# A fused vision tower on one core: the last unit's value products in another buffer, GpSimd's additions behind its last normalisation, output matrices scaled later, far coefficients at the front

## The chip, the cores and the metric

The kernel runs on one core of a Trainium2 chip. The core has a matmul engine (TensorE, PE in the profile), VectorE (DVE), ScalarE (ACT), GpSimd (POOL) and SyncE (SP), whose queue issues the DMAs. The engines run side by side and wait for each other through semaphores. The metric is the device time of one execution in microseconds (us), lower is better. Before the change the median of three runs is 881.12 us (879.34 to 882.15).

## The reference

Everything is float32. Three stages follow one another:

1. A tokenizer over 64 images of 64 channels by 64 x 64 pixels. Each 4 x 4 patch is averaged, `reduce_feats = x.mean((3, 5))`. The averages are normalised and make queries, the 16 pixels of the patch are normalised and make keys and values, and each patch attends to its own 16 pixels with 8 heads: `attn = softmax(q*scale . k)`, `aggre = attn . v`, `h = reduce_feats + aggre @ proj_w.T + proj_b`. That gives 256 tokens of 64 channels for each image.
2. A linear recurrence over the 256 tokens of each image, two states x and z per channel: `x_new = s*x - dsa*z + fx`, `z_new = ds*x + s*z + fz`, with forces made from the tokens by a matrix B. Then `gelu(y @ C + u @ D)`, times its sigmoid, plus the input, and a layer norm.
3. A small network of a shared path and 4 experts of which each token takes 2, and a last layer norm.

## The kernel before

**Units and steps.** Two images lie on the 128 partitions, so the first stage has 32 units (0 to 31), and it is pipelined by hand: step n does the value side of unit n, the key side of unit n + 1 and the first sums of unit n + 2. Each engine has its program written out in the order of its work; nothing is rescheduled. Four units of x fit in `arena`.

**One unit.** GpSimd adds the 16 pixels of each patch in four halvings (lines 497 to 507), after `patch_sums_first` has waited for x. ScalarE makes the means. TensorE makes query means (912, 917), pixel means and squares (924), keys and values (952) into two rings of PSUM. VectorE makes the variance of the queries (`query_var`, 1328), scales them (1333), multiplies keys by queries (`key_products`, 1349) into `prodk`, and scales the scores and takes their maximum (1356, 1363). GpSimd subtracts the maximum (`shift_scores`, 586), ScalarE takes the exponential (`expo`, 708), VectorE sums it (1367) and inverts the sum (1372), GpSimd makes the weights (`weigh_scores` 592, `norm_scores` 597). SyncE spreads them over the channels with eight DMAs into `wbc` (545). VectorE multiplies the values by them (`value_products`, 1380) into `prodv`, four quarters in the order 0, 2, 1, 3; GpSimd adds 4 of the 16 pixels to 4 others (`add_pixels`, 604). TensorE projects the remaining 12 and sums them (`project`, 991), and VectorE adds mean and bias and stores the tokens in `hT` (`tokens`, 1387).

**`prodv` is one buffer.** Value products of unit n wait until `project(n - 1)` has read it (`dve.wait_ge(projected_mm, u)`). In the steady steps projection n - 1 comes before them.

**The second stage begins inside the first.** The tokens are split into halves h = 0 (units 0 to 15) and h = 1. `drive(h, b)` (1006) makes the forces of block b of 4 recurrence steps in four blocks, `forcing` (746) copies them to `z[h]` in SBUF, `scan_ahead` and `scan_on` (1398, 1404) run the recurrence within chunks of L = 16 tokens, and `carry` joins the 16 chunks of an image by four jumps (1449 to 1456), whose steps need powers of the 16-step matrix, `far_steps` (1429, 1432). `scale_out` (738) makes 32 scaled copies of the matrix C with which `from_before` (1100) adds the carried states to the outputs. For h = 0 all of that needs only units 0 to 15, so `drive(0, 0)` to `drive(0, 3)` and part of the scan stand in the last two steps; h = 1 begins when the tokens of unit 31 are there. Step 30 is the last but one: it has keys of unit 31, no sums of a further unit.

**At the start** VectorE prepares constants and does the patch sums of unit 0 itself (483 to 489); GpSimd begins with the patch sums of unit 1 once these are done.

## Time and profile before

| | us |
|---|---|
| median of 3 runs | 881.12 |
| the profiled execution | 881.01 |
| its span on the core | 879.2 |
| PE busy | 838.2 |
| DVE busy | 717.9 |
| POOL busy | 524.4 |
| ACT busy | 483.5 |

The busy time is summed over the whole span. The first stage ends at about 556 us, the recurrence at about 598 us, and the third stage fills the rest. Since each stage has its own limits, the shares of the whole say little of an edit in one place; the order of time around it does. The granted clock of TensorE was 0.99 over the span.

### The profile page before, as it was taken

Reading aid. Unit: us, or ns where it says so; the run is one execution under the profiler, and the core shown is the slowest. Engines: PE = TensorE matmul, PEld = TensorE weight load, DVE = VectorE, ACT = ScalarE, POOL = GpSimd, SP = SyncE. Lnnn points to the kernel's source line nnn. Section 1 sums busy time; section 2 is a strip of 40 time slices with the busy share of each in tenths; the row PEclk is TensorE's granted clock in tenths of the full one; section 3 lists DMA queues with packets and bytes.
Section 4 is the critical chain, followed back from the end, with each engine's and each line's share of the span. In section 5 each row is a group of like instructions: output and inputs, shape, how many; then the busy total and the mean of one; then the engine's idle time right before and its main releaser. Section 6 shows DMA issues by size and latency. Waiting matters only on the chain.

```text
span 879.2 us, 23479 instructions
## 1 busy us (share of the span) xinstructions
PE 838.2 (95%) x9144; PEld 360.6 (41%) x9144; DVE 717.9 (82%) x1189; ACT 483.5 (55%) x782; POOL 524.4 (60%) x387
## 2 busy tenths in 40 slices
PE   5799999999999999999999997898999999999996
PEld 2134334344344343343343443464444444444442
DVE  5788888888888888888888888894788788788785
ACT  3646456455454464564554554358666566566562
POOL 2699999999999999999999964101121121121110
PEclk9999999999999999999999998999999999999999
DMA  9588998989989989999899764000000000000000
GB/s 374 158 240 252 260 283 245 263 267 260 275 250 260 286 242 259 278 250 263 256 253 264 217 168 111 2 2 2 0 13 13 25 13 13 25 13 13 25 13 36
DMA packets 70560, 141.60 MB, mean 161 GB/s; under 512 B 5440, under 2 KB 5440, under 8 KB 69440
## 3 DMA queue, kind: packets, MB, share of 16 engines
q1 hardware_dynamic: 70464, 140.21, 55.4%
q8 instruction: 74, 1.21, 0.6%
q14 instruction: 22, 0.18, 0.1%
HBM read 68.88 MB, written 4.19 MB: 83 GB/s over the span
## 4 chain that ended last, share of the span: by engine, by line
PE 39%; POOL 37%; issue 7%; DVE 7%; ACT 4%; DMA 3%; SPq 2%; POOLq 1%; DVEq 0%; ACTq 0%
POOL sb_rows L497 11%; POOL sb_prodv L604 7%; POOL sb_rows L502 6%; PE ring L1207 5%; POOL sb_wgt L592 4%; PE ring L1177 4%; POOL sb_rows L504 3%; POOL sb_score L586 3%; PE ring L952 3%; PE bank_ms L1219 3%; DMA sb_wbc<-sb_wgt 3%; SPq L545 2%; PE bank_ms L924 2%; PE qp L991 2%; PE qp L1162 2%
## 5 line engine op out<-in xcount | busy, mean ns | idle before, releaser
L952 PE MATMUL ring<-sb_arena,sb_wqkv 64*64 64x512 f32 x2048 | 254.1, 599 | 2.3 <-DVE sb_prodk L1349 1.5
L1380 DVE TENSOR_TENSOR sb_prodv<-ring,sb_wbc 128x1024 f32<-128x1024 f32 x128 | 151.8, 1206 | 43.6 <-DMA sb_wbc<-sb_wgt 25.4
L1349 DVE TENSOR_TENSOR sb_prodk<-ring,sb_qbuf 128x1024 f32<-128x1024 f32 x128 | 150.6, 1218 | 22.3 <-PE ring L952 16.8
L648 POOL TENSOR_TENSOR sb_parts_q<-sb_arena,sb_const 128x512 fp32r<-128x512 f32 x15 | 15.6, 1039 | 245.6 <-DVE sb_arena L1585 194.4
L497 POOL TENSOR_TENSOR sb_rows<-sb_arena 128x2048 f32<-128x2048 f32 x31 | 142.2, 4586 | 15.8 <-DVE sb_sum L489 15.8
L692 ACT ACTIVATE sb_xsq<-sb_arena 128x2048 f32<-128x2048 f32 x64 | 118.6, 1901 | 2.0 <-DMA sb_arena<-x 2.0
L952 PEld LDWEIGHTS ring<-sb_arena,sb_wqkv 64*64 64x64 f32 x2048 | 66.3, 132 | 115.6 <-issue 72.3
L991 PEld LDWEIGHTS qp<-sb_prodv,sb_tok_w 64*64 64x64 f32 x3072 | 93.1, 137 | 40.4 <-issue 40.2
L991 PE MATMUL qp<-sb_prodv,sb_tok_w 64*64 64x128 f32 x3072 | 98.8, 276 | 5.2 <-POOL sb_prodv L604 5.2
L604 POOL TENSOR_TENSOR sb_prodv<-sb_prodv 128x256 f32<-128x256 f32 x128 | 92.8, 735 | 10.7 <-DVE sb_prodv L1380 10.7
L663 ACT ACTIVATE sb_means<-sb_sum 128x256 f32<-128x256 f32 x32 | 13.3, 416 | 146.9 <-POOL sb_sum L507 143.1
L502 POOL TENSOR_TENSOR sb_rows<-sb_rows 128x1024 f32<-128x1024 f32 x31 | 73.9, 2383 | 2.4
L924 PE MATMUL bank_ms<-sb_arena,sb_const 128*32 128x512 f32 x512 | 63.3, 613 | 2.2 <-issue 2.2
L924 PE MATMUL bank_ms<-sb_prodk,sb_const 128*32 128x512 f32 x512 | 61.6, 598 | 1.8 <-DVE sb_prodk L1349 1.8
L924 PE MATMUL bank_sq<-sb_xsq,sb_const 128*32 128x512 f32 x512 | 60.8, 592 | 0.0
L450 ACT ACTIVATE sb_arena<-ring,sb_rest_w 128x512 f32<-128x512 f32 x72 | 49.0, 682 | 7.6 <-PE ring L1167 2.8
L586 POOL TENSOR_TENSOR sb_score<-sb_score,sb_smx 128x512 f32<-128x512 f32 x32 | 40.8, 1276 | 15.8 <-DVE sb_smx L1363 15.4
L1177 PE MATMUL ring<-sb_arena,sb_rest_w 64*128 64x512 f32 x144 | 48.2, 607 | 0.0
L592 POOL TENSOR_TENSOR sb_wgt<-sb_score,sb_rstd 128x512 f32<-128x512 f32 x32 | 41.1, 1285 | 9.9 <-ACT sb_score L708 8.6
L1207 PE MATMUL ring<-sb_prodk,sb_rest_w 128*64 128x512 f32 x192 | 45.9, 598 | 0.0
L673 ACT ACTIVATE sb_qstat<-sb_qstat,sb_const 128x256 f32<-128x256 f32 x32 | 16.3, 509 | 47.1 <-DVE sb_qstat L1328 47.1
L597 POOL TENSOR_TENSOR sb_wgt<-sb_wgt,sb_srz 128x512 f32<-128x512 f32 x32 | 40.9, 1279 | 1.8 <-DVE sb_srz L1372 1.5
(248 smaller groups left out, 1450.1 us busy)
## 6 DMA issues: line engine op xcount, KB each, us to landing
sb_arena<-x SPq DMA_DIRECT2D x64, 1024.0 KB, 7.4
sb_wbc<-sb_wgt SPq DMA_DIRECT2D x256, 256.0 KB, 5.7
out<-sb_arena SPq DMA_DIRECT2D x16, 256.0 KB, 2.0
sb_rest_w<-rest_w SPq DMA_DIRECT2D x1, 950.5 KB, 21.3
sb_const<-const SPq DMA_DIRECT2D x1, 264.5 KB, 3.0
sb_tok_w<-tok_w SPq DMA_DIRECT2D x1, 260.5 KB, 2.9
sb_const<-const SPq DMA_DIRECT2D x1, 256.0 KB, 21.6
```

The lines of the kernel that those rows point to most:

```text
L497: eng.tensor_tensor(rows[:, :, :, :], pix[:, :, 0:8], pix[:, :, 8:16], ALU.add).then_inc(sum8_ready, 1)
L502: eng.tensor_tensor(rows[:, :, 0:4], rows[:, :, 0:4], rows[:, :, 4:8], ALU.add).then_inc(sum4_ready, 1)
L592: pool.tensor_tensor(wgt[:, :], score[:, :], rstd[:, :], ALU.mult).then_inc(weights_raw, 1)
L604: pool.tensor_tensor(part[:, :, N_SUM - N_PRE:N_SUM], part[:, :, N_SUM - N_PRE:N_SUM], part[:, :, N_SUM:N_PIX], ALU.add).then_inc(pixels_a ...
L692: act.activation(xsq[:, half], x[:, m, b].rearrange("p c n -> p (c n)"), ACT.Square).then_inc(pixels_squared, 1)
L924: mm = pe.matmul(bank[32 * c:32 * c + 32, :], what, src[c], start=(b == 0), stop=(b == 1))
L952: mm = pe.matmul(ring[slot][C * half:C * half + C, i, :], image_block(w, i), x[C * i:C * i + C, m, half, c], start=True, stop=True)
L991: mm = pe.matmul(qp[C * i:C * i + C, half, 3 * PT:4 * PT], image_block(projw, half), prodv[rows_of, i, n, :], start=(n == 0), stop=(n == N ...
L1177: pe.matmul(pair[m][:, :], ew1[rows, e, :], h2[rows, i % 3, :], start=True, stop=True).then_inc(ring_mm, 1)
L1207: mm = pe.matmul(bank[C * h:C * h + C, :], ew2[:, 2 * q + h, :], h1e[:, im, 2 * q + h], start=True, stop=True)
L1349: dve.tensor_tensor(by_pixel(prodk[:, c]), by_pixel(ring[c % 2][:, :, :]), q[:, :, None, :].to_broadcast([P, 2, N_PIX, G32]), ALU.mult).th ...
L1380: dve.tensor_tensor(prodv[:, :, :, G32 * c:G32 * (c + 1)], by_pixel(ring[k % 2][:, :, :]), by_pixel(wbc[:, c]), ALU.mult).then_inc(values_ ...
```

## The change

Five edits, all but one in the last two steps of the first stage:

- Unit 31 writes its value products into `prodk` (`products_of`, `prod_last`), whose last user is the scores matmul of unit 31; `project(31)` and the additions read them there. `value_products(31, 0)` waits for `scores_mm` instead of `projected_mm`. TensorE's `project(30)` moves behind `values(31, 1)` and `drive(0, 2)`; VectorE's `tokens(30)` moves behind the first two value products of unit 31.
- GpSimd in step 30: `add_pixels(30, 0)` before `shift_scores(31)`, `add_pixels(30, 1)` between it and `weigh_scores(31)`, and nothing between that and `norm_scores(31)`.
- ScalarE: `scale_out` moves from step 30, ahead of `expo(31)`, to the last step, between the forces of blocks 2 and 3.
- VectorE: the twelve instructions of `far_steps` move from the last step to the front, behind the patch sums of unit 0 and ahead of `query_var(0)`.
- VectorE: ten recurrence steps instead of eight stand ahead of `tokens(31)`: 5 before the first value product, 2 behind the second, 3 behind the fourth.

```diff
@@ gpsimd, step @@
-                if nxt:
+                if nxt and not nxt2:
+                    add_pixels(n, 0)
                     shift_scores(n + 1)
-                add_pixels(n, 0)
-                if nxt:
+                    add_pixels(n, 1)
                     weigh_scores(n + 1)
-                add_pixels(n, 1)
-                if nxt:
                     norm_scores(n + 1)
...
@@ scalar, step @@
                 if not nxt:
-                    forcing(0)
+                    forcing(0, range(N_BLOCK - 1))
+                    scale_out()
+                    forcing(0, range(N_BLOCK - 1, N_BLOCK))
...
-                if nxt and not nxt2:
-                    scale_out()
@@ tensor, last_step @@
                 drive(0, 1)
                 values(n, m, 0)
-                project(n - 1, 0, N_SUM)
                 values(n, m, 1)
                 drive(0, 2)
+                project(n - 1, 0, N_SUM)
                 values(n, m, 2)
@@ vector, value_products @@
                 if k == 0:
-                    dve.wait_ge(projected_mm, u)
-                dve.tensor_tensor(prodv[:, :, :, G32 * c:G32 * (c + 1)], by_pixel(ring[k % 2][:, :, :]),
+                    if isinstance(u, int) and u == UNITS - 1:
+                        dve.wait_ge(scores_mm, UNITS)
+                    else:
+                        dve.wait_ge(projected_mm, u)
+                dve.tensor_tensor(products_of(u)[:, :, :, G32 * c:G32 * (c + 1)], by_pixel(ring[k % 2][:, :, :]),
@@ vector @@
-            EARLY, BEFORE_TOKENS = 5, 9
+            EARLY, BETWEEN, BEFORE_TOKENS = 6, 8, 11
+
+            for level in range(3):
+                far_steps(level)
             query_var(0)
@@ vector, last_step @@
                 for j in range(1, EARLY):
                     scan_ahead(0, j)
                     scan_on(0, j)
-                tokens(n - 1, (m - 1) % NF)
                 value_products(n, m, 0)
                 value_products(n, m, 1)
-                for level in range(3):
-                    far_steps(level)
+                for j in range(EARLY, BETWEEN):
+                    scan_ahead(0, j)
+                    scan_on(0, j)
+                tokens(n - 1, (m - 1) % NF)
                 value_products(n, m, 2)
                 value_products(n, m, 3)
-                for j in range(EARLY, BEFORE_TOKENS):
+                for j in range(BETWEEN, BEFORE_TOKENS):
```

VectorE at the front, before: the last patch sum of unit 0 (`sb_sum`), then the variance and scaling of the first queries and the first key products.

```order
L489 TENSOR_TENSOR sb_sum<-sb_rows 128x128 [waits sum2_ready]
L1328 TENSOR_TENSOR sb_qstat<-qp,sb_qstat 128x256 [waits q_mean_squared]
L1333 TENSOR_TENSOR sb_qraw<-qp,sb_qrstd 128x256 [waits q_ready,q_rstd_ready]
L1349 TENSOR_TENSOR sb_prodk<-ring,sb_qbuf 128x1024 [waits scores_mm,q_ready,keys_mm]
L1349 TENSOR_TENSOR sb_prodk<-ring,sb_qbuf 128x1024 [waits keys_mm]
```

The same place after the change (the twelve instructions go on in the same pattern; `sb_far` holds the powers, `sb_cacc` a temporary).

```order
L495 TENSOR_TENSOR sb_sum<-sb_rows 128x128 [waits sum2_ready]
L1347 TENSOR_SCALAR sb_cacc<-sb_cv,sb_cz 128x2
L1347 TENSOR_SCALAR sb_cacc<-sb_cv 128x2
L1350 SCALAR_TENSOR_TENSOR sb_far<-sb_cz,sb_cacc 128x2 [waits far_step]
L1350 SCALAR_TENSOR_TENSOR sb_far<-sb_cz,sb_cv,sb_cacc 128x2
L1347 TENSOR_SCALAR sb_cacc<-sb_far 128x2 [waits far_step]
```

Between the patch sum and the variance now stand three levels of two `TENSOR_SCALAR` and two `SCALAR_TENSOR_TENSOR`; each of the latter reads two operands in SBUF.

GpSimd from the end of step 29 to the end of its first stage, before (`sb_wgt` holds the weights, `sb_prodv` the value products).

```order
L604 TENSOR_TENSOR sb_prodv<-sb_prodv 128x2x4x32 [waits values_weighted] x2
L586 TENSOR_TENSOR sb_score<-sb_score,sb_smx 128x512 [waits score_max_ready]
L604 TENSOR_TENSOR sb_prodv<-sb_prodv 128x2x4x32 [waits values_weighted]
L592 TENSOR_TENSOR sb_wgt<-sb_score,sb_rstd 128x512 [waits weights_spread2,weights_spread1,weights_spread3,weights_spread0,scores_exp]
L604 TENSOR_TENSOR sb_prodv<-sb_prodv 128x2x4x32 [waits values_weighted]
L597 TENSOR_TENSOR sb_wgt<-sb_wgt,sb_srz 128x512 [waits inverse_sum_ready,weights_raw]
L604 TENSOR_TENSOR sb_prodv<-sb_prodv 128x2x4x32 [waits values_weighted] x6
```

The same place after.

```order
L610 TENSOR_TENSOR sb_prodv<-sb_prodv 128x2x4x32 [waits values_weighted] x3
L592 TENSOR_TENSOR sb_score<-sb_score,sb_smx 128x512 [waits score_max_ready]
L610 TENSOR_TENSOR sb_prodv<-sb_prodv 128x2x4x32 [waits values_weighted]
L598 TENSOR_TENSOR sb_wgt<-sb_score,sb_rstd 128x512 [waits weights_spread2,weights_spread1,weights_spread3,weights_spread0,scores_exp]
L603 TENSOR_TENSOR sb_wgt<-sb_wgt,sb_srz 128x512 [waits inverse_sum_ready,weights_raw]
L610 TENSOR_TENSOR sb_prodv<-sb_prodv 128x2x4x32 [waits values_weighted] x2
L610 TENSOR_TENSOR sb_prodk<-sb_prodk 128x2x4x32 [waits values_weighted] x4
```

The second `sb_wgt` instruction, the normalisation, now follows the first directly, and the four additions of unit 31 work on `sb_prodk`.

VectorE in the last step, before: tokens of unit 30 (`sb_hT`), the first two value products, then the far coefficients.

```order
L1387 SCALAR_TENSOR_TENSOR sb_hT<-qp,sb_bqkv,sb_means 128x16x16 [waits projected_mm]
L1380 TENSOR_TENSOR sb_prodv<-ring,sb_wbc 128x32x32 [waits projected_mm,weights_spread0,values_mm]
L1380 TENSOR_TENSOR sb_prodv<-ring,sb_wbc 128x32x32 [waits weights_spread2,values_mm]
L1429 TENSOR_SCALAR sb_cacc<-sb_cv,sb_cz 128x2
L1429 TENSOR_SCALAR sb_cacc<-sb_cv 128x2
L1432 SCALAR_TENSOR_TENSOR sb_far<-sb_cz,sb_cacc 128x2 [waits far_step]
```

After: the last recurrence step of the middle pair, the tokens of unit 30, and value products 3 and 4 of unit 31.

```order
L1428 SCALAR_TENSOR_TENSOR sb_arena<-sb_arena,sb_sv 128x256 [waits force_ready,scan_step0]
L1434 SCALAR_TENSOR_TENSOR sb_arena<-sb_arena,sb_sv 128x256 [waits scan_step0]
L1417 SCALAR_TENSOR_TENSOR sb_hT<-qp,sb_bqkv,sb_means 128x16x16 [waits projected_mm]
L1410 TENSOR_TENSOR sb_prodk<-ring,sb_wbc 128x32x32 [waits weights_spread1,values_mm]
L1410 TENSOR_TENSOR sb_prodk<-ring,sb_wbc 128x32x32 [waits weights_spread3,values_mm]
```

The tokens moved from ahead of the first value product to between the second and the third, and the far coefficients are gone from there.

## Rows read from the trace of the kernel before

**Rows 1.** the page, the chain that ended last, shares of the span by engine

```profile
PE 39%; POOL 37%; issue 7%; DVE 7%; ACT 4%; DMA 3%; SPq 2%; POOLq 1%; DVEq 0%; ACTq 0%
```

**Rows 2.** stretches: busy us (instructions) by engine, granted clock, DMA share, GB/s

```profile
300.00:316.00 16.00, 16.00 (x232) 6.55 (x227) 13.77 (x17) 8.39 (x12) 15.39 (x12) 1.00 0.91 262
551.00:556.00 5.00, 4.52 (x96) 4.30 (x96) 3.20 (x8) 0.00 (x0) 0.26 (x2) 0.66 0.01 3
```

**Rows 3.** GpSimd in order of time at the front: start us, us, instruction, idle before

```profile
16.27 4.53 POOL L497 TENSOR_TENSOR sb_rows<-sb_arena 128x2048 f32<-128x2048 f32 x1 [15.82 <-DVE sb_sum L489]
20.87 2.37 POOL L502 TENSOR_TENSOR sb_rows<-sb_rows 128x1024 f32<-128x1024 f32 x1
23.32 1.27 POOL L504 TENSOR_TENSOR sb_rows<-sb_rows 128x512 f32<-128x512 f32 x1
...
30.88 1.27 POOL L586 TENSOR_TENSOR sb_score<-sb_score,sb_smx 128x512 f32<-128x512 f32 x1 [5.47 <-DVE sb_smx L1363]
```

**Rows 4.** VectorE in order of time at the front

```profile
15.82 0.29 DVE L489 TENSOR_TENSOR sb_sum<-sb_rows 128x128 f32<-128x128 f32 x1
19.24 0.42 DVE L1328 TENSOR_TENSOR sb_qstat<-qp,sb_qstat 128x256 f32<-128x256 f32 x1 [3.12 <-ACT sb_qstat L669]
```

**Rows 5.** VectorE in order of time, the far coefficients in the last step

```profile
545.17 0.22 DVE L1429 TENSOR_SCALAR sb_cacc<-sb_cv 128x2 f32<-128x2 f32 x1
545.42 0.57 DVE L1432 SCALAR_TENSOR_TENSOR sb_far<-sb_cz,sb_cacc 128x2 f32<-128x2 f32 x1
545.91 0.21 DVE L1432 SCALAR_TENSOR_TENSOR sb_far<-sb_cz,sb_cv,sb_cacc 128x2 f32<-128x2 f32 x1
```

**Rows 6.** GpSimd in order of time, the last units

```profile
501.78 1.28 POOL L597 TENSOR_TENSOR sb_wgt<-sb_wgt,sb_srz 128x512 f32<-128x512 f32 x1
...
528.87 1.27 POOL L586 TENSOR_TENSOR sb_score<-sb_score,sb_smx 128x512 f32<-128x512 f32 x1 [8.51 <-DVE sb_smx L1363]
...
534.12 1.28 POOL L597 TENSOR_TENSOR sb_wgt<-sb_wgt,sb_srz 128x512 f32<-128x512 f32 x1
535.35 1.77 POOL L604 TENSOR_TENSOR sb_prodv<-sb_prodv 128x256 f32<-128x256 f32 x2
...
545.20 0.77 POOL L604 TENSOR_TENSOR sb_prodv<-sb_prodv 128x256 f32<-128x256 f32 x1 [0.40 <-DVE sb_prodv L1380]
...
550.03 0.89 POOL L604 TENSOR_TENSOR sb_prodv<-sb_prodv 128x256 f32<-128x256 f32 x1 [0.40 <-DVE sb_prodv L1380]
```

**Rows 7.** VectorE in order of time, the last units

```profile
509.16 1.23 DVE L1380 TENSOR_TENSOR sb_prodv<-ring,sb_wbc 128x1024 f32<-128x1024 f32 x1 [0.31 <-DMA sb_wbc<-sb_wgt]
...
532.17 1.04 DVE L1367 TENSOR_REDUCE sb_ssm<-sb_score 128x32 f32<-128x512 f32 x1 [1.03 <-ACT sb_score L708]
533.24 0.35 DVE L1372 RECIPROCAL sb_srz<-sb_ssm 128x32 f32<-128x32 f32 x1
...
534.59 1.09 DVE L1398 SCALAR_TENSOR_TENSOR sb_arena<-sb_arena,sb_sv 128x256 f32<-128x256 f32 x1
...
542.27 0.67 DVE L1387 SCALAR_TENSOR_TENSOR sb_hT<-qp,sb_bqkv,sb_means 128x256 f32<-128x256 f32 x1 [2.63 <-PE qp L991]
...
547.60 2.35 DVE L1380 TENSOR_TENSOR sb_prodv<-ring,sb_wbc 128x1024 f32<-128x1024 f32 x2
...
555.64 0.65 DVE L1387 SCALAR_TENSOR_TENSOR sb_hT<-qp,sb_bqkv,sb_means 128x256 f32<-128x256 f32 x1 [1.69 <-PE qp L991]
```

**Rows 8.** one line of the scan: durations ns, first and last start us

```profile
L1398 DVE SCALAR_TENSOR_TENSOR sb_wbc<-sb_wbc,sb_sv x14: 477/485/489, 569.7 to 581.6; 128x256 f32<-128x256 f32 x14
```

**Rows 9.** ScalarE in order of time, the last two steps

```profile
523.88 7.74 ACT L738 ACTIVATE sb_arena<-sb_rest_w,sb_cz 128x64 f32<-128x64 f32 x32
531.53 0.61 ACT L708 ACTIVATE sb_score<-sb_score 128x512 f32<-128x512 f32 x1
```

**Rows 10.** TensorE in order of time, last projection and end of the scan

```profile
551.07 4.52 PE L991 MATMUL qp<-sb_prodv,sb_tok_w 64*64 64x128 f32 x96 [3.94 <-POOL sb_prodv L604]
...
590.38 1.87 PE L1100 MATMUL ring<-sb_xsq,sb_arena 64*64 64x128 f32 x60 [1.96 <-DVE sb_xsq L1456]
```

More of the change, by code:

```diff
@@ L198, in image_block, with products_of @@
             return w[C * i:C * i + C, C * i:C * i + C]
+        prod_last = prodk[:, :, :, :].rearrange("p c i n -> p (c i n)").rearrange("p (i n t) -> p i n t", i=2, n=N_PIX)
+        def products_of(u):
+            return prod_last if isinstance(u, int) and u == UNITS - 1 else prodv
         x = arena[:, :].rearrange("p (m b c n) -> p m b c n", m=NF, b=2, c=NC)
@@ L738, in scale_out, with forcing @@
                         act.activation(dst[:, j], out_mat, ACT.Copy, scale=cz[:, j + 1, o:o + 1]).then_inc(scaled_out, 1)
-            def forcing(h):
+            def forcing(h, blocks):
                 act.wait_ge(coefs, N_COEFS)
-                for b in range(N_BLOCK):
+                for b in blocks:
                     act.wait_ge(drive_mm, N_BLOCK * h + b + 1)
@@ L771, in _ @@
             pipeline(act, step, UNITS)
-            forcing(1)
+            forcing(1, range(N_BLOCK))
             def norm_sq(i):
@@ L1324, in _, with far_steps, last @@
             first_patch_sums(dve, 1)
+            def far_steps(level):
+                def last(acc):
+                    return (cz, cv)[acc][:, L] if level == 0 else far[:, acc, level - 1]
+                if level > 0:
+                    dve.wait_ge(far_step, 4 * level)
+                for acc in range(2):
+                    dve.tensor_scalar(cacc[:, acc, 0], last(1), last(acc)[:, 1:2], None, ALU.mult).then_inc(far_step, 1)
+                dve.wait_ge(far_step, 4 * level + 2)
+                for acc in range(2):
+                    dve.scalar_tensor_tensor(far[:, acc, level], last(0), last(acc)[:, 0:1], cacc[:, acc, 0],
+                                             ALU.mult, ALU.add).then_inc(far_step, 1)
             def query_var(u):
```

24 lines of the change are left out of this document (11 added, 13 removed).

## The prediction

> **What bounds the kernel now.** I read first the chain that ended last by engine: TensorE and GpSimd share it, the others have little [rows 1]. Then stretches. In a steady stretch of 16 us GpSimd is busy 15.39 us, and TensorE counts as busy throughout while its matmuls are pipelined [rows 2]; so in the first stage GpSimd has almost no slack, and a delay of its first unit is not made up later. Third, the order of time of GpSimd and VectorE at the front [rows 3, 4] and of all engines in the last two steps [rows 5 to 10]. There the reader is to see a chain of short waits: ScalarE's exponential of unit 31 stands behind 32 scalings [rows 9], VectorE sits idle for the projection of unit 30 before it may overwrite `prodv` (2.63 us) and again for the projection of unit 31 (1.69 us) [rows 7], and TensorE waits 3.94 us for the last addition and 1.96 us for the last carry [rows 10].
>
> The sum is made on the profiled execution: 881.01 us, which is its span of 879.2 and 1.8 around it, and 0.11 below the median of the runs shown. Times below are on the clock of the trace of before; the delay at the front, where there is one, shifts all that follows alike and is added at the end.
>
> **The exponential and the normalisation, 1.5 us.** `shift_scores(31)` ends at 528.87 + 1.27 = 530.14 [rows 6], but the exponential begins at 531.53, behind scalings that took 7.74 us from 523.88 [rows 9]. With these moved it runs 530.2 to 530.8. VectorE's sum of it had 1.03 us of idle ahead of it [rows 7], so VectorE was free at 531.14: sum and reciprocal come 1.03 earlier and end at 533.24 + 0.35 - 1.03 = 532.56. Before, the normalisation did not start on the reciprocal's end (533.59) but at 534.12, behind an addition; now nothing is between. It starts at 532.6, 1.5 us earlier, and ends at 533.9. The two additions that now stand before it (0.73 each) lie in the wait for the scores' maximum, 8.51 us [rows 6], and beside the exponential.
>
> **The spread of the weights sets the first value product.** Its price is in unit 29, where no wait but the DMA's stood before the product: normalisation over at 501.78 + 1.28 = 503.06 [rows 6], product at 509.16, released by the DMA [rows 7]: 6.1 us. So `value_products(31, 0)` can start at 533.9 + 6.1 = 540.0 and not before. It started at about 542.8 (tokens of unit 30 from 542.27, after the projection). The freed buffer thus brings 2.8 us, no more, and VectorE has a new idle of about 1 us for the DMA, because five recurrence steps from 533.5 at 0.915 us each ((581.6 - 569.7) / 13 [rows 8]), with some waits for GpSimd, end at about 539.0.
>
> **From there to the last projection, 2.9 us.** Two value products 2.35 [rows 7], two recurrence steps 1.83 and 0.2 for one wait behind an addition, tokens of unit 30 (0.5 to the next start), two products 2.35: 540.0 + 7.2 = 547.2. Before, the last pair began at 547.60 and ended at 549.95, and the projection started at 551.07, 1.1 later. Now it starts at 548.2, 2.9 earlier. TensorE's projection of unit 30 is finished long before 544 in either case, since its additions end at about 535.5.
>
> **The recurrence, 1.8 us more.** Ten steps instead of eight are ahead of the tokens of unit 31, so 2 x 0.915 = 1.83 us are gone from VectorE's work behind them. VectorE is busy from 555.64 until it releases TensorE at 590.38. TensorE had 1.96 us of slack there [rows 10] and its own work starts with the tokens too, so the gain is the smaller of 1.83 and 1.96. Together the last steps give 2.9 + 1.8 = 4.7 us. The scalings, now behind the forces of block 2 (copied by about 537.6: the exponential's end at 530.8 and then three blocks, each some 2.2 us of matmuls and copying), run to 545.3 and the forces of block 3 to 546.8; the first matmul of half 1 wants them at about 553.6, so they cost nothing; without that cover they cost up to their 7.74.
>
> What of the 4.7 is loose: the last projection took 4.52 us, and the granted clock was 0.66 over 551 to 556 [rows 2], so about 0.34 x 5 / 0.5 = 3.4 us of it were at the lower of the two levels. All at the upper, it would be 1.7 shorter; all at the lower, about 1.1 longer. I leave it as it was. With 0.5 for the other starts, the gain is 3.3 to 6.5.
>
> **The far coefficients at the front, a loss of 5.7 us.** Their own time is about 2.6 us (the second of the twelve started at 545.17, the value products behind them at 547.60 [rows 5, 7], one more ahead), and they go into a gap of 3.12 us ahead of the first query variance [rows 4]: by that alone they are free. But two rows show what a `SCALAR_TENSOR_TENSOR` with both operands in SBUF does beside GpSimd. At 545.42 one on 2 elements took 0.57 us and its twin 0.21; GpSimd's addition ran 545.20 to 545.97, and the first of the two ended at 545.99 [rows 5, 6]. At 534.59 a recurrence instruction took 1.09 instead of 0.485; GpSimd's normalisation ended at 535.40, and it ended 0.28 after that [rows 6 to 8]. Each waited for GpSimd's running instruction to end. At the front GpSimd starts its patch sum of unit 1 at 16.27, for 4.53 us [rows 3]. VectorE's last patch sum ends at 16.11, its first `SCALAR_TENSOR_TENSOR` of the far steps would start 0.3 us later at 16.4, the same distance as at 545.12 to 545.42, so after GpSimd again. It waits until 20.80. Its twin passes in the gap to 20.87. Level 1 needs two short instructions first, meets the second patch sum (20.87, 2.37) and waits until about 23.3; level 2 meets the third (23.32, 1.27) and waits until about 24.7; two short ones more and `query_var(0)` starts at 24.9 instead of 19.24: 5.7 us late. Behind it hang the query's scaling, the key products, the scores and `shift_scores(0)`, for which GpSimd had been idle 5.47 us waiting on VectorE [rows 3], so the whole delay arrives there, and with GpSimd at 15.39 of 16 us nothing takes it back.
>
> The nearest rows bound this loss on both sides: 0 if no such wait arises, and for the upper end VectorE losing every gap until GpSimd runs out of patch sums at about 25.4, plus two free levels of 0.8 (2.4 us for three [rows 5, 7]): 27.0, or 7.8 us late. I take 5.7 because both rows show VectorE getting in as soon as GpSimd's instruction ends.
>
> The rule in the Trainium skill, page "SBUF — State Buffer", section "Who interferes with whom", goes further than these rows: besides VectorE instructions with two SBUF inputs it names `tensor_scalar` from SBUF to SBUF, in a two-port mode, as one that shares the port pair with GpSimd and blocks or is blocked for a whole instruction. No row here shows that for a `TENSOR_SCALAR`: the one at 545.17 was already running. By that rule it would come out as the second rival.
>
> **Sum.** 881.01 - 4.7 + 5.7 = 882.0 us. A difference under 0.3%, 2.6 us, is what this kernel's measurement cannot tell from none; the forecast is within it.
>
> **Rivals.**
> - No block at the front. The far steps fit the 3.12 us gap, VectorE's first one beats GpSimd to it, or the waits are short. For it: a margin of only 0.13 us between GpSimd's start (16.27) and VectorE's. Against it: the same margin at 545.2 did not help. Time: 881.0 - 4.7 = 876.3, faster.
> - VectorE loses more gaps: also its `TENSOR_SCALAR` instructions wait. Level 1's pair waits for 23.3 and its next for 24.7, level 2's for 25.5, and 0.8 us later, at 26.3, the variance starts: 7.1 late, 7.8 at the bound. Time: 881.0 - 4.7 + 7.1 = 883.4, up to 884.1, slower. It decides from the point where one level more than in my count is left over when GpSimd's third sum ends.
> - The moved scalings turn into the wait. If block 2's forces come only behind the projection, the scalings start near 548 and block 3's forces end at 557.2, and drive and recurrence of half 1 begin there. This leaves a gain of 0.8 instead of 4.7, and 881.0 - 0.8 + 5.7 = 885.9, slower. It decides from a start of the scalings after 544.3; TensorE's `drive(0, 2)` stands ahead of the projection, which speaks against it.
>
> **How the numbers follow.** Forecast 0.60, no block 0.16, more gaps lost 0.20, scalings 0.04. The likeliest one's own range is 880 to 883.6 (gain 3.3 to 6.5, loss 5.6 to 6). The whole range, 876.0 to 884.3, takes in the first two rivals. Faster by over 2.6 us is almost only the no-block case and a lucky clock: 0.17. Slower by over 2.6 (from 883.7): half of the second rival, all of the third and a little of the forecast: 0.17. The same: 0.66.
>
> **What would show it.** At the front: the first `SCALAR_TENSOR_TENSOR` of the far steps lasting over 4 us and ending with GpSimd's first patch sum, `query_var(0)` near 24.9, and every later start of GpSimd's patch sums 5.7 us later than before; if it stands at 19.2, that step is wrong and 876 follows. In the last steps: the normalisation of unit 31 1.5 us nearer to its score maximum, an idle of about 1 us of VectorE for the weights' DMA, no idle for the projection of unit 30, the last projection starting 15.6 us after the start of that normalisation (551.07 - 534.12 = 16.95 before), and TensorE's 1.96 us before the last `from_before` almost gone. The forecast is wrong if first-stage delays are absorbed between the units, or if the last projection finds the clock at another level for all of its length.

## The result and the profile after

| | kernel before | changed kernel |
|---|---|---|
| time, median | 880.59 us (878.81 to 882.73, 7 runs) | 884.71 us (883.27 to 888.05, 7 runs) |
| ratio, 95% interval | | 1.0055 (1.004 to 1.007) |
| profiled execution, span | 879.2 us | 881.5 us (883.27 us in all) |
| measured again (e16 below) | 880.15 us | 884.21 us, 1.0050 (1.0036 to 1.0065) |

It is slower by 4.1 us. I had forecast 882.0 us, no measurable difference, and at most 884.3. The profiled execution is the fastest of the seven, so its differences to before (+2.3 us) understate the median; where the rest lies is shown with e16.

In the chain by engine GpSimd and VectorE each hold three points less than in [rows 1] and TensorE seven more:

```profile
PE 46%; POOL 34%; issue 8%; DVE 4%; DMA 3%; SPq 2%; ACT 2%; POOLq 1%; DVEq 0%
```

The front, VectorE in order of time (start us, us, instruction, idle before), answering to [rows 4]:

```profile
16.39 4.39 DVE L1350 SCALAR_TENSOR_TENSOR sb_far<-sb_cz,sb_cacc 128x2 f32<-128x2 f32 x1
20.70 0.21 DVE L1350 SCALAR_TENSOR_TENSOR sb_far<-sb_cz,sb_cv,sb_cacc 128x2 f32<-128x2 f32 x1
20.94 2.40 DVE L1347 TENSOR_SCALAR sb_cacc<-sb_far 128x2 f32<-128x2 f32 x2
23.38 1.30 DVE L1350 SCALAR_TENSOR_TENSOR sb_far<-sb_far,sb_cacc 128x2 f32<-128x2 f32 x2
24.72 0.77 DVE L1347 TENSOR_SCALAR sb_cacc<-sb_far 128x2 f32<-128x2 f32 x2
...
25.79 0.42 DVE L1355 TENSOR_TENSOR sb_qstat<-qp,sb_qstat 128x256 f32<-128x256 f32 x1
```

and GpSimd, answering to [rows 3]:

```profile
16.24 4.52 POOL L503 TENSOR_TENSOR sb_rows<-sb_arena 128x2048 f32<-128x2048 f32 x1 [15.79 <-DVE sb_sum L495]
20.83 2.36 POOL L508 TENSOR_TENSOR sb_rows<-sb_rows 128x1024 f32<-128x1024 f32 x1
23.27 1.26 POOL L510 TENSOR_TENSOR sb_rows<-sb_rows 128x512 f32<-128x512 f32 x1
24.61 0.72 POOL L513 TENSOR_TENSOR sb_sum<-sb_rows 128x256 f32<-128x256 f32 x1
38.23 1.28 POOL L592 TENSOR_TENSOR sb_score<-sb_score,sb_smx 128x512 f32<-128x512 f32 x1 [12.90 <-DVE sb_smx L1390]
```

Read the two side by side. The first `SCALAR_TENSOR_TENSOR` ends at 20.78, GpSimd's first sum at 20.76. Level 1's two `TENSOR_SCALAR`s end at 23.34, GpSimd's second sum at 23.19; the pair of `SCALAR_TENSOR_TENSOR`s at 24.68 and the third sum at 24.53; level 2's `TENSOR_SCALAR`s at 25.49 and the fourth sum at 25.33. So at each of GpSimd's four ends the waiting pair gets through, and the next pair starts 0.11 us after the next sum has begun (20.94 against 20.83, 23.38 against 23.27, 24.72 against 24.61) and has to wait for it. `query_var(0)` starts at 25.79, 6.55 us late. GpSimd's first shift starts at 38.23, 7.35 us late: the other 0.8 us is TensorE's, which had no matmul from 22.5 to 29.6; its granted clock fell to the lower of its two levels at 25.8 (0.50, which is 1.2 of 2.4 GHz), and it began the key products there. The stretches of the idle and of the key products, engines' busy us and granted clock as in [rows 2]:

```profile
20.00:28.00 8.00, 2.47 (x24) 0.42 (x16) 6.49 (x12) 1.19 (x3) 5.09 (x4) 0.86 0.81 334
28.00:32.00 4.00, 2.39 (x12) 0.75 (x16) 3.29 (x4) 1.41 (x3) 0.00 (x0) 0.50 0.02 4
```

The tail, on GpSimd (answering to [rows 6]), VectorE [rows 7] and TensorE [rows 10]:

```profile
524.18 1.28 POOL L603 TENSOR_TENSOR sb_wgt<-sb_wgt,sb_srz 128x512 f32<-128x512 f32 x1 [0.18 <-DVE sb_srz L1399]
...
539.89 1.27 POOL L603 TENSOR_TENSOR sb_wgt<-sb_wgt,sb_srz 128x512 f32<-128x512 f32 x1 [0.39 <-DVE sb_srz L1399]
...
555.81 0.90 POOL L610 TENSOR_TENSOR sb_prodk<-sb_prodk 128x256 f32<-128x256 f32 x1 [0.40 <-DVE sb_prodk L1410]
```

```profile
532.73 1.22 DVE L1410 TENSOR_TENSOR sb_prodv<-ring,sb_wbc 128x1024 f32<-128x1024 f32 x1 [1.38 <-DMA sb_wbc<-sb_wgt]
...
548.46 2.35 DVE L1410 TENSOR_TENSOR sb_prodk<-ring,sb_wbc 128x1024 f32<-128x1024 f32 x2 [2.13 <-issue]
...
553.40 2.33 DVE L1410 TENSOR_TENSOR sb_prodk<-ring,sb_wbc 128x1024 f32<-128x1024 f32 x2
...
559.76 0.65 DVE L1417 SCALAR_TENSOR_TENSOR sb_hT<-qp,sb_bqkv,sb_means 128x256 f32<-128x256 f32 x1 [0.94 <-PE qp L1004]
...
564.98 0.42 DVE L1446 TENSOR_TENSOR sb_xsq<-sb_arena 128x256 f32<-128x256 f32 x1
```

```profile
543.11 2.80 PE L1004 MATMUL qp<-sb_prodv,sb_tok_w 64*64 64x128 f32 x96
549.74 3.69 PE L965 MATMUL ring<-sb_arena,sb_wqkv 64*64 64x512 f32 x16 [3.83 <-DVE sb_prodk L1410]
...
556.85 2.85 PE L1004 MATMUL qp<-sb_prodk,sb_tok_w 64*64 64x128 f32 x96 [1.78 <-POOL sb_prodk L610]
```

How late each is against before, in us: normalisation of unit 30 +6.47 (524.18 against 517.71), normalisation of unit 31 +5.77, first value product of unit 31 +5.68, last pair of them +5.80, last projection +5.78, tokens of unit 31 +4.12, end of the recurrence +2.28 (564.98 against 562.70), end +2.3. So the last normalisation gained 1.58 on the 7.35; nothing more was gained up to the last projection; the projection itself took 2.85 instead of 4.52 because here it found the full clock (the lower level lay from 548.1 to 554.9, ahead of it, and in before from 551.8 to 555.3, across it); and the two recurrence steps moved ahead gave 1.84. The last projection starts 16.96 us after the start of that normalisation; I had said 15.6, and before it was 16.95.

### The profile page after: what moved, and what is told of

Read it like the earlier page. It is cut to its first block, busy times and chain, and to the rows that moved or that the text cites. A ratio compares the mean times of both kernels' runs of the same rounds, so it can differ in the third digit from the quotient of the medians.

```text
span 881.5 us, 23480 instructions
## 1 busy us (share of the span) xinstructions
PE 836.6 (95%) x9144; PEld 357.6 (41%) x9144; DVE 725.1 (82%) x1189; ACT 483.6 (55%) x782; POOL 524.5 (60%) x387
## 4 chain that ended last, share of the span: by engine, by line
PE 46%; POOL 34%; issue 8%; DVE 4%; DMA 3%; SPq 2%; ACT 2%; POOLq 1%; DVEq 0%
POOL sb_rows L503 11%; POOL sb_rows L508 6%; POOL sb_prodv L610 6%; PE ring L965 6%; PE ring L1220 5%; PE ring L1190 4%; POOL sb_rows L510 3%; POOL sb_wgt L598 3%; PE bank_ms L937 3%; PE bank_ms L1232 3%; POOL sb_score L592 3%; DMA sb_wbc<-sb_wgt 3%; PE qp L1004 2%; PE qp L1175 2%; SPq L551 2%
## 5 line engine op out<-in xcount | busy, mean ns | idle before, releaser
L1410 DVE TENSOR_TENSOR sb_prodv<-ring,sb_wbc 128x1024 f32<-128x1024 f32 x124 | 147.1, 1206 | 43.7 <-PE ring L965 24.9
L661 POOL TENSOR_TENSOR sb_parts_q<-sb_arena,sb_const 128x512 fp32r<-128x512 f32 x15 | 15.6, 1039 | 243.7 <-DVE sb_arena L1604 194.4
L1004 PEld LDWEIGHTS qp<-sb_prodv,sb_tok_w 64*64 64x64 f32 x2976 | 86.6, 133 | 33.7 <-issue 33.7
L610 POOL TENSOR_TENSOR sb_prodv<-sb_prodv 128x256 f32<-128x256 f32 x124 | 89.9, 735 | 7.2 <-DVE sb_prodv L1410 7.2
L1004 PE MATMUL qp<-sb_prodv,sb_tok_w 64*64 64x128 f32 x2976 | 92.2, 269 | 0.0
```

The lines of the kernel that those rows point to most:

```text
L610: pool.tensor_tensor(part[:, :, N_SUM - N_PRE:N_SUM], part[:, :, N_SUM - N_PRE:N_SUM], part[:, :, N_SUM:N_PIX], ALU.add).then_inc(pixels_a ...
L1004: mm = pe.matmul(qp[C * i:C * i + C, half, 3 * PT:4 * PT], image_block(projw, half), products_of(u)[rows_of, i, n, :], start=(n == 0), sto ...
L1410: dve.tensor_tensor(products_of(u)[:, :, :, G32 * c:G32 * (c + 1)], by_pixel(ring[k % 2][:, :, :]), by_pixel(wbc[:, c]), ALU.mult).then_in ...
```

## The experiments

Medians; the ratio is to runs of the kernel before on the same chip, with its 95% interval. "Gap" is the place ahead of `score_scale(0)`, where VectorE waits 2.05 us for TensorE and GpSimd is idle. The runs of one kernel scatter by 2 to 11 us, and the intervals are 2 to 5 us wide, so differences under about 2 us between two kernels are not settled by the medians; smaller ones are read from the traces. The twelve instructions, 1.3 us in the expectations, take 2.3 us by themselves (e5).

| run | far coefficients | tail | us | ratio |
|---|---|---|---|---|
| e1 | last step | changed | 878.17 | 0.9976 (0.9961 to 0.9992) |
| e2 | front | before | 886.17 | 1.0064 (1.0045 to 1.0083) |
| e3 | gap | changed | 875.56 | 0.9944 (0.9928 to 0.9960) |
| e4 | gap | before | 878.33 | 0.9981 (0.9966 to 0.9996) |
| e5 | front, GpSimd held | changed | 874.54 | 0.9942 (0.9915 to 0.9970) |
| e6 | level 0 front, rest gap | changed | 877.72 | 0.9964 (0.9941 to 0.9987) |
| e7 | last step | products only | 880.02 | 0.9997 (0.9978 to 1.0015) |
| e8 | last step | additions, scaling only | 878.35 | 0.9973 (0.9961 to 0.9985) |
| e9 | gap | scalings last | 876.71 | 0.9963 (0.9949 to 0.9977) |
| e10 | gap | additions as before | 876.53 | 0.9946 (0.9929 to 0.9964) |
| e11 | gap | recurrence 7, 2, 2 | 873.85 | 0.9926 (0.9905 to 0.9946) |
| e12 | gap | scalings last, 5, 3, 3 | 877.92 | 0.9978 (0.9963 to 0.9993) |
| e13 | gap | transfers by chunk | 877.23 | 0.9972 (0.9961 to 0.9983) |
| e14 | gap | by chunk, 5, 2, 4 | 879.28 | 0.9991 (0.9975 to 1.0008) |
| e15 | gap | scaling as before | 876.59 | 0.9967 (0.9951 to 0.9984) |
| e16 | front | changed | 884.21 | 1.0050 (1.0036 to 1.0065) |

**e1, e2, e3, e4: the front against the tail.** Of the kernels e1 and e3 have the changed tail, e2 and e4 that of before. The place of three lines is all that differs:

```diff
@@ e3: the changed kernel, VectorE
-            for level in range(3):
-                far_steps(level)
             query_var(0)
 ...
             key_products(0, 0, 3)
+            for level in range(3):
+                far_steps(level)
             score_scale(0)
@@ e1: instead, in last_step, behind value_products(n, m, 1)
+                for level in range(3):
+                    far_steps(level)
```

> The changed kernel with the far coefficients back in the last step, behind the second value product; everything else as changed. Theory A (the front costs 6.5 to 7.3 us and the tail gains about 3 to 4): query_var(0) starts at 19.2 again and the time is 880.6 - 3.5 = about 877.1 (876.3 to 878.2). Rival B (the tail itself lost, by the slower transfer of the weights and the clock, and the stretch of stage 1 had taken back most of the front's loss): the time is 880 to 883.

> The kernel before with only the far coefficients moved to the front, ahead of query_var(0). Theory A: query_var(0) 6.5 late, GpSimd's first shift 7.3 late, and of that 0 to 0.9 taken back over stage 1; the last step saves the 1.3 us of the twelve instructions at most: 880.6 + 6.4 less 0 to 1.3 = 885.7 to 887.0. Rival B (stage 1 absorbs): 881 to 883.

> The changed kernel with the twelve instructions of the far coefficients between the first unit's last key product and its score_scale, where VectorE waits 2.05 us for TensorE and GpSimd is idle. Theory A: they take 1.3 us of those 2.05 us, nothing is late at the front, and the time is 876 to 878, by up to 1.3 us below the one with the coefficients in the last step. Rival C (any TENSOR_SCALAR chain at the front costs its own length): 878 to 879. Rival B: 880 to 883.

> The kernel before with only the far coefficients moved, to the same gap ahead of score_scale(0). Theory A: nothing lost at the front; in the last step 1.3 us of VectorE's work goes, but there it lay between the second value product and the wait for the third's sums, so it gains 0 to 1.3: 879.3 to 880.6. If the place at the front costs by itself, over 881.

Theory A holds, B falls: the tail alone is 2.1 us faster, the front alone 5.9 us slower. The front costs more against the gap, since the last step is rid of the twelve instructions in both: 7.8 us with the tail as before (e4 to e2), 9.1 with the changed tail (e3 to the changed kernel). Three places of the same twelve instructions with the tail as before: 886.2, 880.3 (the kernel before) and 878.3; with the changed tail: 884.7, 878.2 and 875.6. C falls as well: in the gap they cost nothing, `score_scale(0)` starts 9.89 us after `query_var(0)` in e3 and 9.81 in before. In e2's trace TensorE's granted clock was 0.50 for all of 28 to 38, longer than in the changed kernel's, and the first shift was 9.5 us late, not 7.35. The profile is of e2's longest run, so this is its upper end (VectorE, query variance and score scale):

```profile
25.99 0.42 DVE L1342 TENSOR_TENSOR sb_qstat<-qp,sb_qstat 128x256 f32<-128x256 f32 x1
...
38.56 0.69 DVE L1370 TENSOR_TENSOR sb_score<-bank_ms,sb_rstd 128x512 f32<-128x512 f32 x1 [3.76 <-PE bank_ms L924]
```

**e5: is it GpSimd?** One wait on GpSimd, ahead of its first patch sums:

```diff
+            pool.wait_ge(far_step, 12)
             patch_sums_first(pool, 1, 1)
```

> The changed kernel, far coefficients at the front as changed, but GpSimd waits for the twelfth of them before it starts its first patch sums. Theory A (what costs is GpSimd's running additions and nothing else): the twelve instructions take 2.1 us in all (0.2 each), GpSimd starts near 18.1 instead of 16.2 and ends its sums by 27.1, still ahead of its first shift at 30, query_var(0) starts by 19.2 and the time is that of the kernel with the coefficients in the gap, 875.6 (875 to 877). Rival D (GpSimd's late start is passed on, one for one): 877.3 to 878. Rival E (the place at the front costs by itself, whatever GpSimd does): 883 to 885.

```profile
16.36 0.22 DVE L1351 SCALAR_TENSOR_TENSOR sb_far<-sb_cz,sb_cacc 128x2 f32<-128x2 f32 x1
...
16.75 0.36 DVE L1348 TENSOR_SCALAR sb_cacc<-sb_far 128x2 f32<-128x2 f32 x2
17.14 0.35 DVE L1351 SCALAR_TENSOR_TENSOR sb_far<-sb_far,sb_cacc 128x2 f32<-128x2 f32 x2
...
18.89 0.43 DVE L1356 TENSOR_TENSOR sb_qstat<-qp,sb_qstat 128x256 f32<-128x256 f32 x1 [0.61 <-ACT sb_qstat L683]
```

The same instructions at the same place take 0.2 us each, 2.3 us in all, and fit the gap of 3.12 us; `query_var(0)` starts at 18.89. The time is that of e3. So the whole loss is GpSimd running beside them, D and E fall, and GpSimd's later start (18.36) costs nothing that shows.

**e6: one level.** `far_steps(0)` at the front, levels 1 and 2 in the gap.

> The changed kernel with only the first level of the far coefficients (four instructions) at the front, the other two levels in the gap ahead of score_scale(0). Theory A: the first SCALAR_TENSOR_TENSOR ends with GpSimd's first sum, at 20.8, query_var(0) starts at 21.0 instead of 18.5 to 19.2, 1.8 to 2.5 us late: 877.4 to 878.2 against 875.6 with all in the gap. Rival: each instruction pays a share of the 6.5 us (a third for a third): 2.2 us as well, but then spread over the four and not in the first.

```profile
16.38 4.48 DVE L1350 SCALAR_TENSOR_TENSOR sb_far<-sb_cz,sb_cacc 128x2 f32<-128x2 f32 x1
...
20.92 0.41 DVE L1355 TENSOR_TENSOR sb_qstat<-qp,sb_qstat 128x256 f32<-128x256 f32 x1
```

One instruction pays for all of it, 4.48 us. The median is 2.2 us above e3 as expected, but GpSimd's first shift was 5.1 us later than in e3 (35.32 against 30.20) though `query_var(0)` was only 2.44 later: TensorE, starved again, worked on the key products at a granted clock of 0.50 from 26 to 32. Its runs scatter from 873.3 to 883.2, and the profile (881.2) is from near the top of that range.

**e7, e8: the tail in its two parts.** e7 is before with `products_of`, the order of TensorE's `last_step` and the recurrence in 5, 2, 3 steps; e8 is before with the order of GpSimd's additions and the moved `scale_out` only (all as in the change's diff).

> The kernel before with only the products' part: the last unit's products in prodk, tokens(30) and project(30) behind the first two value products, two recurrence steps moved ahead; GpSimd's additions, the scaling and the far coefficients as before. If the first value product of the last unit is then bound by the transfer of the weights (7.3 us after the normalisation at 535.4, as in the changed kernel's trace), it starts at 542.7, where it started at 542.78 before: nothing there, and only the 1.8 us of the recurrence steps: 880.3 - 1.8 = 878.5. If the transfer takes 5.8 us, it starts at 541.2 and 1.5 us more come: 877.0. Forecast 877.0 to 878.8.

> The kernel before with only GpSimd's additions moved behind and ahead of the last normalisation and the scaling moved later; products, order and far coefficients as before. The last normalisation starts 1.5 us earlier, and since project(30) waits for GpSimd's additions behind it, tokens(30) and the first value product come 1.5 us earlier too, if the weights' transfer allows: 880.3 - 1.5 = 878.8. If the gain needs the new buffer, 880.3. Both parts together and no far coefficients moved were 878.2, so one of the two parts brings nothing on top of the other.

```profile
538.71 2.36 DVE L1403 TENSOR_TENSOR sb_prodk<-ring,sb_wbc 128x1024 f32<-128x1024 f32 x2 [0.46 <-issue]
540.99 0.22 DVE L1340 TENSOR_SCALAR sb_cacc<-sb_cv,sb_cz 128x2 f32<-128x2 f32 x1
...
545.25 0.65 DVE L1410 SCALAR_TENSOR_TENSOR sb_hT<-qp,sb_bqkv,sb_means 128x256 f32<-128x256 f32 x1
545.74 2.33 DVE L1403 TENSOR_TENSOR sb_prodk<-ring,sb_wbc 128x1024 f32<-128x1024 f32 x2
...
553.92 0.65 DVE L1410 SCALAR_TENSOR_TENSOR sb_hT<-qp,sb_bqkv,sb_means 128x256 f32<-128x256 f32 x1 [2.77 <-PE qp L997]
```

The early normalisation alone brings 1.7 us (e8). The buffer with its two recurrence steps brings nothing that the medians show (e7, where the interval leaves room for 1.9 us), and nothing on top of the early normalisation (e1, 878.2 against 878.35). e7's trace says why the buffer brings nothing. The first value product starts early, 5.60 us after the normalisation's end (533.11), but what follows it on VectorE is now the far coefficients (2.56 us) and two recurrence steps, and then the second pair starts 12.6 us after the normalisation's end where it was 12.2 in before. Without the far coefficients there the changed tail brings 2.8 us (e4 to e3), but that is not the buffer either: the last pair starts 12.2 us after the normalisation in e3 and 11.1 in e4, which has the old buffer. By their traces the gain is the normalisation 1.5 us nearer to its shift, the two recurrence steps, and a last projection of 2.85 us against 5.40, less this 1.1. The 2.1 and 2.8 us of the tail with and without the coefficients in it do not differ beyond the scatter.

**e9, e10, e15: which edit makes the normalisation early, and what does the scaling cost?**

```diff
@@ e9: e3, ScalarE in the last step
-                    forcing(0, range(N_BLOCK - 1))
-                    scale_out()
-                    forcing(0, range(N_BLOCK - 1, N_BLOCK))
+                    forcing(0, range(N_BLOCK))
+                    scale_out()
```

e10 is e3 with GpSimd's additions, e15 e3 with ScalarE's scaling as in the kernel before.

> The changed kernel with the far coefficients in the gap ahead of score_scale(0), and the 32 scalings of the output matrices behind all four blocks of forces, not ahead of the last. In the changed kernel's trace the first value product of the last unit started 7.3 us after the normalisation's end, in the runs with the scalings elsewhere 5.6 to 5.8. Theory F (the scalings beside the weights' transfer hold it up): it starts 5.6 to 5.8 us after, the idle of 2.1 us is gone, and the time is up to 1.5 us below the 875.6 of the same kernel with the scalings ahead of the last block: 874.1 to 875. Theory G (the transfer's own scatter, or another cause in the order): 7.3 again and 875.6. Both if the scalings' 7.7 us do not delay the forces of half 1.

> The changed kernel with the far coefficients in the gap, and GpSimd's additions in the order of before (shift, add, weigh, add, normalise). The exponential is early here, the additions stand between again. By the trace of before an addition took 0.73 and the normalisation waited behind one; by the forecast's count 0.5 of the 1.5 us of the normalisation's gain comes from the additions (534.12 against the reciprocal's end at 533.59) and 1.0 from the scalings: 875.6 + 0.5 = 876.1, and no more than 877.1. If the additions are all of it: 877.1.

> The changed kernel with the far coefficients in the gap and the scalings back where they were before, ahead of the exponential of unit 31. The exponential then waits for them: the normalisation of unit 31 1.0 us later (1.03 us of idle of VectorE ahead of the sum, in the trace of before). Theory: 875.6 + 1.0 = 876.6. If the first value product then starts 5.7 us after the normalisation instead of 7.3, that gives back 1.5: 875.0 to 875.6.

From the start of the shift to the start of the normalisation of unit 31 it is 3.81 us in e3, 3.92 in e10 and 4.87 in e15 (5.25 in before): put back alone, the scaling costs 1.1 and the additions 0.1, not 0.5, and both together 1.4. So the moved scaling brings nearly all of it, and the moved additions bring 0.4 only where the scaling stays (5.25 to 4.87). Kernels with both edits scatter from 3.66 to 3.95, so the 0.1 is not told from nothing. Theory F falls: with no scaling beside the transfer the first value product of e9 still starts 7.3 us after the normalisation (540.70 against 533.43), and the late scaling makes TensorE wait 1.33 us for the forces of half 1. e15 surprised: its normalisation is later, but the product starts 5.66 us after it, so both come out within a microsecond.

```profile
540.16 2.36 DVE L1410 TENSOR_TENSOR sb_prodk<-ring,sb_wbc 128x1024 f32<-128x1024 f32 x2 [0.50 <-issue]
```

**e13, e14: the order of the transfers.** SyncE issues four transfers for a pair of chunks; e13 swaps its two loops, e14 adds one recurrence step behind the last value product.

```diff
-                    for i in range(2):
-                        for c in VALUE_ORDER[k:k + 2]:
+                    for c in VALUE_ORDER[k:k + 2]:
+                        for i in range(2):
```

> The changed kernel with the far coefficients in the gap, and the four transfers of a pair of chunks issued chunk by chunk (both halves of the first chunk, then both of the second) instead of half by half. Theory H (the first value product of the last unit waits for the third of four transfers to land, and that is the 7.3 us): it is now the second of four, one issue of 0.75 us and about 1 us of transfer earlier, so the product starts by 5.6 us after the normalisation, the idle of 2.1 us shrinks to under 0.5, and the time is 0 to 1.5 us under 875.6. Rival (the wait is not for the transfer): 7.3 again, 875.6.

> As the one before, and one recurrence step more behind the last value product, ahead of the tokens of unit 31 (four where three were). It needs the forces of block 3, there by about 549. VectorE had 0.9 to 2.6 us of idle ahead of those tokens, so the step of 0.92 us is free: 0.9 below the time of the one before. If the forces of block 3 are late, nothing.

```profile
541.16 1.22 DVE L1410 TENSOR_TENSOR sb_prodk<-ring,sb_wbc 128x1024 f32<-128x1024 f32 x1
544.41 1.23 DVE L1410 TENSOR_TENSOR sb_prodk<-ring,sb_wbc 128x1024 f32<-128x1024 f32 x1 [2.04 <-DMA sb_wbc<-sb_wgt]
...
548.22 2.34 DVE L1410 TENSOR_TENSOR sb_prodk<-ring,sb_wbc 128x1024 f32<-128x1024 f32 x2
```

```profile
545.69 1.99 PE L965 MATMUL ring<-sb_arena,sb_wqkv 64*64 64x512 f32 x8 [2.17 <-DVE sb_prodk L1410]
...
551.68 4.52 PE L1004 MATMUL qp<-sb_prodk,sb_tok_w 64*64 64x128 f32 x96 [2.54 <-POOL sb_prodk L610]
```

Theory H is right on the wait and wrong on its worth. The first product starts 5.07 us after the normalisation (536.09), without idle: it did wait for the transfer. But the second waits until 8.3 us, as late as in e4, TensorE idles in between and falls to the lower level (eight matmuls 1.99 instead of 1.09, the projection 4.52 instead of 2.85), and the time is 1.7 us worse than e3. e14 is unclear: in its trace the recurrence ends 24.4 us after the normalisation against 25.4 in e13, the microsecond that was expected at that place, but its median is 2 us above e13's. Part of the answer is under e11: a third extra step arrives at TensorE as 0.3 us. Where the rest went is not shown.

**e11, e12: a better version.** `EARLY, BETWEEN, BEFORE_TOKENS` is 8, 10, 12 in e11 (before it 6, 8, 11); 6, 9, 12 with e9's scaling in e12.

> The changed kernel with the far coefficients in the gap and the recurrence of half 0 moved further ahead: 7 steps before the first value product (5 as changed), 2 before the tokens of unit 30 (2), 2 behind the last value product (3), so that one more is done before the tokens of unit 31. Two of the steps fit the idle of 2.1 us ahead of the first value product (1.83 us). If that idle is a wait and not time that VectorE itself needs, nothing else moves and the end of the recurrence comes 0.92 us earlier: 875.6 - 0.9 = 874.7. If the last projection or the forces of block 3 are late, 875.6; if the idle was not free, 877.4.

> The two together: far coefficients in the gap, scalings behind all forces, recurrence 5, then 3, then 3 steps. By theory F the first value product starts 1.5 us earlier and three steps fit ahead of the tokens of unit 30: 873 to 874.5. By theory G 874.7 to 876.

```profile
540.35 2.36 DVE L1410 TENSOR_TENSOR sb_prodk<-ring,sb_wbc 128x1024 f32<-128x1024 f32 x2 [0.32 <-issue]
...
545.28 2.34 DVE L1410 TENSOR_TENSOR sb_prodk<-ring,sb_wbc 128x1024 f32<-128x1024 f32 x2
...
551.65 0.65 DVE L1417 SCALAR_TENSOR_TENSOR sb_hT<-qp,sb_bqkv,sb_means 128x256 f32<-128x256 f32 x1 [1.85 <-PE qp L1004]
...
555.96 0.42 DVE L1446 TENSOR_TENSOR sb_xsq<-sb_arena 128x256 f32<-128x256 f32 x1
```

e11 has the lowest median: 5.7 us under the 879.55 of the kernel before on the same chip, 0.74%, and faster than both kernels. That it is faster than e3 is not shown: the intervals overlap (0.9905 to 0.9946 against 0.9928 to 0.9960). The idle ahead of the first value product shrank from 2.10 to 0.32 us while the product stood where it was, 7.32 us after the normalisation, and the recurrence ends 22.9 us after it, 0.9 less than in e3 (23.8). Of this 0.9 only 0.3 reaches TensorE. From the start of the tokens of unit 31 to the first `from_before` it is 34.74 us in before, 32.88 in e3 and 32.58 in e11 and e14: the first two recurrence steps moved ahead used up the 1.96 us that TensorE waited there [rows 10], and after them its own matmuls set the time. e12 puts a third step ahead of the tokens of unit 30, where nothing is idle: the tokens, the drives behind them and the last projection are late.

**e16: the changed kernel again.**

> The changed kernel unchanged, measured once more beside the kernel before: 884.7 against 879.5 to 880.6, ratio 1.0055 (1.004 to 1.007). If the last projection is at the full clock in one run and at half in another, the runs lie in two groups about 1.5 to 3 us apart.

Two groups, as in the first measurement: four runs of 882.5 to 884.6, two of 886.7 and 888.1. The profiled one is the slowest, 4.8 us above the profile of the first section. Of that 0.6 is there at the last normalisation (541.75 against 541.16), 1.7 comes in the last projection (4.52 us against 2.85), and 2.4 between the recurrence's end (567.35) and the program's. There the two traces differ in the granted clock, first e16, then the changed kernel's first profile:

```profile
850.00:887.00 37.00, 28.32 (x127) 12.13 (x123) 20.89 (x47) 12.34 (x25) 0.00 (x0) 0.84 0.08 29
```

```profile
850.00:882.00 32.00, 22.91 (x117) 10.95 (x115) 19.38 (x41) 11.64 (x24) 0.00 (x0) 0.96 0.07 25
```

## Why the prediction was wrong

The mechanism at the front, VectorE waiting for GpSimd's running sums, was right; which instructions it catches, and so its size, was not. The time lay 0.4 us above my range.

- **"Level 1 needs two short instructions first" is the step that failed.** I let only the `SCALAR_TENSOR_TENSOR`s wait and the `TENSOR_SCALAR`s pass beside a running sum: 5.7 us. In [rows 5] no `TENSOR_SCALAR` met a running addition, so no row showed it free either. The trace shows them waiting for whole sums (2.40 us for two, 0.36 in e5), and `query_var(0)` came 6.55 late. This is my second rival (7.1), to which I gave 0.20, and what the Trainium skill, page "SBUF — State Buffer", section "Who interferes with whom", says of `tensor_scalar`; the trace agrees: 25.79, against the rival's 26.3 and my 24.9. I should have given the rule more weight, since no row spoke against it.
- **The delay grew after VectorE.** I passed 5.7 us on one for one. It grew by 0.8 us here (0.7 in e16's trace) and by 2.7 in e6, 2.8 in e2 (query 6.75, shift 9.51 late), both in profiles near the top of their kernels' ranges, and in all four TensorE, starved, came back at half clock. This term was missing from all cases.
- **"Nothing takes it back": nearly right.** 0.88 of 7.35 was back at the normalisation of unit 30, but one step later, at unit 31's shift, 7.35 again.
- **Normalisation 1.5 us earlier:** 1.58. Its parts were mis-shared: I gave the scaling 1.0 and the additions 0.5, and put back alone they cost 1.1 and 0.1 (e15, e10).
- **Transfer 6.1 us: mis-sized.** It was 7.3 in the changed kernel, so of the 1.4 us that the freed buffer was to bring up to the last projection, nothing came (5.77 late, then 5.78). My price was one instance, unit 29 of the kernel before, and the spread has more than one (below): one unit earlier in the same trace the product starts 7.3 us after its normalisation, not 6.1.
- **Recurrence 1.83:** 1.84. Last projection: I left it at 4.52; in two traces of the same kernel it is 2.85 and 4.52, within what I had allowed for the clock, so which one a run has was not forecast by anything here.
- **Scalings cost no wait:** right. The rival of no block at the front is excluded by the trace.

By terms measured in the changed kernel's trace, the last projection left at 4.52: 881.0 - 1.6 - 0 - 1.8 + 7.35 = 884.9, against a median of 884.7. So read, my tail gain of 4.7 was 3.4, my loss of 5.7 was 7.35, and both errors have one sign. The medians share it out otherwise: e3, the changed tail with nothing lost at the front, is 4.7 us under before, my own figure (3.5 to 6.3 by its interval), and the front then costs about 9. e3's profile has the short projection (1.7 us) and its first query 0.8 us earlier than before, which the trace terms leave out. That the loss at the front was too small holds either way; how the tail's gain is to be counted stays open by about 1.3 us.

Why did the same eight transfers release the first value product after 5.6 to 5.8 us in e2, e4, e7, e8 and e15 and after 7.2 to 7.4 in the changed kernel, e1, e3, e5, e6 and e9 to e12? It is not the scaling's work beside them (e9), the additions (e10) or VectorE's recurrence (e11). The landing times in the traces answer most of it. A transfer lands in 16 parts. The third of the eight, which completes the first chunk, has 15 parts down by 5.6 us after the normalisation in every one of these kernels; the 16th follows by 5.8 or lands at 7.2 to 7.4, and the value product starts 0.1 us after it. In that time one other thing runs on the DMA engines, a load of 16 KB of program. In e3 it starts 5.14 us after the normalisation and takes 0.97 us (DMA queue 8, window 537.60 to 537.70):

```profile
q8 instruction: 1, 0.02, 60.4%
```

In e7 and e15 the load comes at 5.7 us, too late to touch either of the first two chunks (second chunk landed at 6.6 and 6.7). In e2, e4 and e8 it comes at 5.3 and holds back one part of the fourth transfer and not of the third (first chunk 5.7, second 8.3). In the other kernels, at 5.1 to 5.3, one part of both is late. The start alone does not decide which. Over the 32 units of the 16 kernels that issue the transfers in this order, where no load started between 1 us before the normalisation's end and 5.5 us after it, the third transfer never had a part more than 1 us behind the others (0 of 33); where one started 2 to 3.5 us after, it always had (82 of 82). The price in the prediction has the same origin: in unit 29 of before 15 parts were down at 5.4 us and the 16th at 6.0, with a load from 4.96; in unit 28, with a load from 4.15, the 16th landed at 7.2. That a load on the same DMA engine holds the part back is inferred from these times: no run moved a load on purpose, the traces do not name the DMA engine of a part, and why the loads fall where they do in each kernel is not shown.

The buffer could not have brought much in any case: the third chunk lands 10.9 to 11.1 us after the normalisation in all of these kernels and the last pair started 12.2 after it in before, so little over 1 us was to be had at the last pair.

That the clock caused the rest of the two groups of run times is read from two traces, not tested.

## What to carry to other kernels

A gap of VectorE is free only for instructions that can run beside what GpSimd does in it: look at GpSimd in the same microseconds, and count each dependent pair of small instructions with SBUF operands as one whole GpSimd instruction. Put such a chain where GpSimd waits; here that turned +4.1 us into -4.7. Filling VectorE's idle as well (-5.7 by the median) is not shown to add more than 0.3, because TensorE's slack behind it was already used up: a step moved ahead is worth what the engine that waits for it still waits. A delay of a few microseconds that starves TensorE at the start costs more than itself, and a buffer that is freed earlier pays only up to the next limit, here the landing of the third chunk, and only if what stands behind it on the engine is not longer than what it saved.

## What the hardware showed that I had not expected

- Tiny instructions (128 partitions x 2 elements, 0.2 us alone) took up to 4.57 us beside GpSimd, `TENSOR_SCALAR` no less than `SCALAR_TENSOR_TENSOR`: one dependent pair per GpSimd instruction.
- One load of 16 KB of program, 0.96 us long, beside eight transfers of 256 KB held back a single one of the 16 parts of a transfer by about 1.7 us, and the engine that waited for all 16 with it (first chunk 7.2 instead of 5.5 us). Whether the first chunk, the second or neither is hit changed from kernel to kernel with edits that have nothing to do with the transfers.
- Idle that the profile puts down to "issue" was a wait for a DMA: in e3 2.10 us before the first value product, which starts 0.08 us after the last part of its chunk has landed.
- The granted clock of the last 37 us was 0.84 in one run of a kernel and 0.96 over the last 32 in another: 2.4 us, with no edit near it.
